# Column sums of a linear-attention kernel: one burst after each job, or one pair of matmuls after every second tile of the next job

## What is computed

```python
xn = layernorm(x)
q, k, v = split(xn @ W_qkv.T)            # 16 heads of 128
q = elu(q) + 1; k = elu(k) + 1
out = q * cumsum(k * v) / (q * cumsum(k) + 1e-9)     # over the 16,384 tokens
x = x + layernorm(out @ W_out.T * 128**-0.5)
# feed-forward, hidden 2048, inner 8192
f = silu((xn2 @ w_gate) * s_gate) * ((xn2 @ w_up) * s_up)    # xn2 = layernorm(x)
x = x + layernorm((f @ w_down) * s_down)
```

## Time and profile before

| | us |
|---|---|
| median of 2 runs | 10222.65 (10217.5 to 10227.79) |
| the profiled execution | 10219.21 |
| its span, core 0 (slowest) | 10217.6 |
| its span, core 4 (fastest) | 10086.5 |

### The profile page before, as it was taken

The page is one execution under the profiler, slowest core; times in us unless marked ns, Lnnn a source line. Parts: engine busy times, 40 slices in busy tenths (PEclk is TensorE's granted clock), DMA queues, the critical chain, the costliest instruction groups (busy, mean ns, idle before and its releaser), DMA issues.

```text
span 10217.6 us, 92396 instructions; the slowest of 8 cores (10086.5 to 10217.6 us)
## 1 busy us (share of the span) xinstructions
PE 7937.6 (78%) x33524; PEld 3392.3 (33%) x34200; DVE 2220.8 (22%) x3267; ACT 2050.9 (20%) x2825; POOL 492.5 (5%) x497
## 2 busy tenths in 40 slices
PE   0898687886868868688686885555599899899897
PEld 0343233332323323233232331111244344344343
DVE  3331231222313223132231111333210110210101
ACT  1222222222322323233231221121100000100100
POOL 0000000000000000000000000000011111111110
PEclk9999888888888888888887986666799999999998
DMA  4653433324333243332433113222697896995994
GB/s 114 147 115 59 111 82 72 83 53 100 81 75 85 59 97 82 70 87 63 97 82 62 26 26 78 87 87 80 107 153 148 165 152 150 162 157 155 157 145 140
DMA packets 1214500, 1034.29 MB, mean 101 GB/s; under 512 B 385330, under 2 KB 1089843, under 8 KB 1187123
## 3 DMA queue, kind: packets, MB, share of 16 engines
q0 software_dynamic: 759504, 587.23, 35.1%
q1 hardware_dynamic: 85412, 348.80, 9.8%
q10 hardware_dynamic: 369152, 92.31, 5.1%
HBM read 749.06 MB, written 153.35 MB: 88 GB/s over the span
## 4 chain that ended last, share of the span: by engine, by line
PE 73%; DMA 10%; ACTq 6%; ACT 4%; issue 3%; DVE 3%; another core or an unknown queue 1%; SPq 0%; DVEq 0%; POOLq 0%
PE psq L54 41%; PE ps_z L54 9%; PE ps_g L54 8%; PE ps_u L54 8%; DMA ts_st<-tsrow 6%; ACTq L54 6%; PE ps_at L54 2%; ACT tsrow L54 2%; PE ps_kvc L54 1%; PE ps_kc L54 1%; PE psts L54 1%; DVE ln_s L54 1%; DMA xb<-x_sh 1%; DMA q_st<-qbuf 1%
## 5 line engine op out<-in xcount | busy, mean ns | idle before, releaser
L54 PE MATMUL psq<-wqb,xnT 128*128 128x512 bf16 x19054 | 4274.1, 384 | 437.0 <-DMA xnT<-xn_st 372.6
L54 PEld LDWEIGHTS psq<-wqb,xnT 128*128 128x128 bf16 x19456 | 1921.1, 99 | 2808.2 <-issue 582.7
L54 PE MATMUL ps_g<-ynT,wgb 128*128 128x512 bf16 x4014 | 935.0, 383 | 154.7 <-DVE fuse L54 104.4
L54 PE MATMUL ps_u<-ynT,wub 128*128 128x512 bf16 x4014 | 919.9, 379 | 4.3
L54 PE MATMUL ps_z<-wdb,fuse 128*128 128x512 bf16 x4015 | 891.8, 382 | 33.9 <-DVE zf L54 19.7
L54 DVE SCALAR_TENSOR_TENSOR kbuf<-psq,r2b 128x512 bf16<-128x512 f32 x576 | 398.0, 691 | 2385.9 <-ACT r2b L54 2385.9
L54 ACT COPY tsrow<-psts 1x1024 f32<-1x1024 f32 x512 | 491.5, 998 | 1623.6 <-issue 776.9
L54 DVE SCALAR_TENSOR_TENSOR kvbuf<-psq,kbuf 128x512 bf16<-128x512 f32 x576 | 397.9, 691 | 1841.9 <-PE psq L54 1828.2
L54 PE MATMUL psts<-kvbuf,u_sb 128*1 128x512 bf16 x512 | 206.1, 520 | 696.2 <-ACT tsrow L54 695.5
L54 ACT ACTIVATE r2b<-psq 128x512 f32<-128x512 f32 x640 | 380.9, 595 | 1350.9 <-PE psq L54 1338.6
L54 PEld LDWEIGHTS ps_g<-ynT,wgb 128*128 128x128 bf16 x4096 | 403.9, 99 | 647.8 <-issue 175.1
(11 more groups left out here) (58 smaller groups left out, 2007.8 us busy)
## 6 DMA issues: line engine op xcount, KB each, us to landing
wqb<-wqkvT POOLq DMA_DIRECT2D x76, 2048.0 KB, 17.2
xb<-x_full SPq DMA_DIRECT2D x128, 1024.0 KB, 4.9
wgb<-wg POOLq DMA_DIRECT2D x128, 1024.0 KB, 6.9
wub<-wu POOLq DMA_DIRECT2D x128, 1024.0 KB, 9.3
wdb<-wd POOLq DMA_DIRECT2D x128, 1024.0 KB, 5.1
xn_st<-xnb SPq DMA_DIRECT2D x144, 512.0 KB, 2.8
xb<-x_sh SPq DMA_DIRECT2D x16, 1024.0 KB, 6.1
xrb<-x_sh SPq DMA_DIRECT2D x16, 1024.0 KB, 5.9
```

Source lines behind the costliest of these rows:

```text
L54: ins = getattr(e, meth)(*args, **kw)
```

## The change

The sums of a job are no longer recorded behind its tiles. Each group of two (two `psts` matmuls, the copy, the DMA) becomes a function that remembers its buffer, column and the two eviction counts it waits for, and is put on a list, `st.pending_ts`. In the next job, one group is taken from the list behind each tile after which `st.gidx` is odd, that is behind its tiles 0, 2, ..., 14; background steps stay behind the odd tiles. At the last job of a pass the whole list, which then holds that job's eight groups, is emptied after `tail_hook`. The waits of a group are the same, with the parity of the buffers taken when it is emitted. `P1State` gets a constructor.

```diff
--- before.py
+++ after.py
@@ -247,8 +247,10 @@
                 p0_tile(x_src, row0, tt, dst_st, xbuf, xnb, ln_done, dxp2, dxnp2)
 
         class P1State:
-            gidx = 0
-            ts_group = 0
+            def __init__(self):
+                self.gidx = 0
+                self.ts_group = 0
+                self.pending_ts = []
 
         mev_hist = {}
 
@@ -318,6 +320,8 @@
 
                     mev_hist[st.gidx] = mev_now
                     st.gidx += 1
+                    if st.pending_ts and st.gidx % 2 == 1:
+                        st.pending_ts.pop(0)()
                     if bg and st.gidx % 2 == 0:
                         bg.pop(0)()
 
@@ -326,17 +330,21 @@
                     tail_hook = None
                 if ts_base is not None and kind in ("k", "v"):
                     tbuf = kbuf if kind == "k" else kvbuf
-                    for tt in range(NTT):
-                        gpar = st.ts_group % 2
-                        TE.wait(C["mev"], mev_hist[st.gidx - NTT + tt])
-                        if tt % 2 == 0 and st.ts_group >= 2:
-                            TE.wait(C["mtse"], st.ts_group - 1)
-                        TE.op("matmul",
-                              ps_ts[gpar][0:1, (tt % 2) * 512:(tt % 2) * 512 + 512],
-                              u_sb[:, 127:128],
-                              tbuf[:, tt * 512:(tt + 1) * 512],
-                              start=True, stop=True, inc=(C["mts"], 1))
-                        if tt % 2 == 1:
+                    for t0 in range(0, NTT, 2):
+                        def ts_group_emit(t0=t0, tbuf=tbuf, kind=kind, col=col,
+                                          base=ts_base,
+                                          mevs=(mev_hist[st.gidx - NTT + t0],
+                                                mev_hist[st.gidx - NTT + t0 + 1])):
+                            gpar = st.ts_group % 2
+                            for j, tt in enumerate((t0, t0 + 1)):
+                                TE.wait(C["mev"], mevs[j])
+                                if j == 0 and st.ts_group >= 2:
+                                    TE.wait(C["mtse"], st.ts_group - 1)
+                                TE.op("matmul",
+                                      ps_ts[gpar][0:1, j * 512:j * 512 + 512],
+                                      u_sb[:, 127:128],
+                                      tbuf[:, tt * 512:(tt + 1) * 512],
+                                      start=True, stop=True, inc=(C["mts"], 1))
                             dtsp = C["dts0"] if gpar == 0 else C["dts1"]
                             SC.wait(C["mts"], C["mts"].n)
                             SC.wait(dtsp, dtsp.n)
@@ -345,14 +353,17 @@
                             st.ts_group += 1
                             SY.wait(C["mtse"], ev)
                             idx = 0 if kind == "k" else 1
-                            g0 = ts_base + tt - 1
                             SY.op("dma_start",
-                                  out=ts_st[idx:idx + 1, g0:g0 + 2,
+                                  out=ts_st[idx:idx + 1, base + t0:base + t0 + 2,
                                             col:col + 512],
                                   in_=tsrow[gpar][0:1, :].rearrange(
                                       "p (g j) -> p g j", j=512),
                                   inc=(dtsp, 16))
-
+                        st.pending_ts.append(ts_group_emit)
+
+                if ji0 == len(jt_list) - 1:
+                    while st.pending_ts:
+                        st.pending_ts.pop(0)()
                 if do_stash:
                     buf = {"k": kbuf, "v": kvbuf, "q": qbuf}[kind]
                     stg = {"k": k_st, "v": kv_st, "q": q_st}[kind]
```

## The result

| us | before | after |
|---|---|---|
| profiled execution | 10219.21 | 9410.47 |
| its span, slowest core | 10217.6 (core 0) | 9408.9 (core 2) |
| spans of the eight cores | 10086.5 to 10217.6 | 9383.0 to 9408.9 |
| lowest of all runs | 10204.51 (10 runs) | 9405.67 (11 runs) |
| median of all runs | 10516.53 | 9842.65 |

The ratio of after to before is 0.9206, 95% interval 0.9182 to 0.9231: 7.9% less time. Both medians hold executions in which the four cores of one die, or all eight, were granted a lower TensorE clock on average; the ratio and the times of the experiments leave these cores out.

A forecast was written before the change was run, and what follows sets the result against it. TensorE bound the kernel, idling before `psts` for copies `tsrow` and their DMAs. 10,219 − 1,023 (56 bursts) − 68 (cold restarts) + 278 (448 pairs) = 9,406 us; range 9,310 to 9,590.

The forecast's parts named there:

- a pair: Two `psts` matmuls after every second tile of the next job: 0.62 us each, 448 of them adding 278 us.
- switching: TensorE going from full matmuls to `psts` and back: 0.10 and 0.09 us per pair.
- a pass's end: Last job of a pass, sums still emptied behind the transposes: 66 us, unchanged; 465 us over eight stay.
- rival B: Inside passes, all cores dense: clock lowered; at 0.81 the whole gain of 813 us goes, near 10,220; chance 0.04.
- Rivals A and C: A: pairs dearer, 9,769 at 1.43 us each, chance 0.12. C: copy and DMA set the pace, 10,430 or more, 0.03.
- the ring: Copy into `tsrow`, then DMA out, two buffers: 14.1 us between uses against some 8.2 at worst, so nothing waits.
- Rival D: At a pass's end: transposes late for want of `xn_st`, at most some 57 us a pass, some 9,810; chance 0.03.
- The cover: Copies on ScalarE and DMAs on SP, moved into the next job, fit in slack: cost nothing, ScalarE about 41% busy.
- The sum: Profiled execution: 10,219 − 1,023 (56 bursts) − 68 (their cold restarts) + 278 (448 pairs) = 9,406 us.
- The spread: Across cores: core 0 stays slowest, core 4 gains some 80 us less, ending near 9,355; 131 narrows to about 50 us.
- cold restart: TensorE resuming at a lower clock after a burst inside a pass: 1.2 us each, 56 removed, 68 us.

## Why the prediction came out as it did

The mechanism and its size were right: at full clock the changed kernel takes 9,406 to 9,421 us, where 9,406 was forecast. The median of all runs, 9,843, is 253 us above the range.

| step | predicted | measured |
|---|---|---|
| a pair | 0.62 us | 0.627 |
| of it, switching | 0.19 | 0.20 (one matmul behind every tile) |
| a job with its pairs | 60.2 | 60.28 |
| a pass | 544 | 544.7 (1080.99 to 1625.65) |
| idle before `psts` | 420 | 411 |
| clock inside a pass | 0.98 or more | 1.00 |
| a pass's end | 66, unchanged | 65.0; across seven ends 121.7 against 121.8 |
| waits of copies for DMAs between tiles | none | none (24 waits, three at each flush) |
| slowest core, spread | core 0, 50 us | core 2, 26 us |

*The step that failed* is the one that made the sum into a forecast of the median: "the median of the runs shown is 10,223, 4 us above that execution, so I leave it at 9,406". It let three executions that agreed stand for all. The range was then built from the kernel's own mechanisms only. The clock entered as an outcome of the change (rival B, 0.04), not as something that befalls either kernel from one execution to the next, though it moves the changed kernel's time by up to 1,057 us (9,405.67 to 10,462.75). The runs show it in both kernels. Of the changed kernel 8 of 11 executions took 9,534 us or more, each with one die or both at a lower clock. Of before 5 of 10 took 10,780 or more; their clocks weren't kept, but executions of before beside the experiments show the same (11,574 us with all cores at 0.76 to 0.77). The median execution of the changed kernel shows both clocks side by side: cores 0 to 3 ran at a granted clock of 0.914 on average and ended at 9,391 to 9,403, cores 4 to 7 at 0.87 and ended at 9,814 to 9,841. The two medians, 10,517 and 9,843, stand at 0.936, where the ratio at full clock is 0.921.

*Rival B* as written, that density brings the lower clock and eats the gain, isn't borne out: in four executions of the changed kernel the average is 0.91, up from 0.875 to 0.88, and the own pass stays at 1.00. Whether density makes the lower clock more frequent, 8 of 11 and 5 of 10 can't tell. But the sentence that the trace of the own pass disagrees with the page was too strong. In another execution, of the kernel with one row buffer, the own pass of core 4 ran at 0.82, beside 0.99 at the same place before:

```profile
302.00:816.00 514.00, 507.20 (x1938) 210.44 (x1939) 160.19 (x248) 117.70 (x176) 7.99 (x7) 0.82 0.48 109
```

1,938 matmuls stand where before has 2,339. The Trainium skill, "TensorE: Matmul & The Clock Gate", Part 1, "Seeing it yourself", gives 13/16 (0.81) for dense matmuls on three or more cores of a die. This row agrees with the level. That it holds whenever three cores are dense doesn't agree: in the profiled execution of the changed kernel the same stretch is at 1.00 on each of the eight cores, all dense. What sets it off wasn't found.

*Rivals A and C* are closed: the switch was measured in two ways (one matmul behind every tile, four behind every fourth), and the ring has room even with half its buffers. *Rival D* didn't come: the passes' ends are as long as before.

*The cover* on which the moved copies were costed at nothing held. ScalarE is busy 147 us in 450, a third rather than the 41% worked out; the stretch holds four v jobs, which need it little, and three k jobs.

*The sum, and the luck in it.* The sum was made on core 0. There the eight passes, up to the first matmul of the prefix sums, took 5,120.1 us before (from 1079.81) and 4,308.0 after (from 1064.75): 812 less, where 813 was forecast. The first row is of before, the second of the changed kernel:

```profile
6199.86 8.35 PE L54 MATMUL ps_pre<-tssb,ps_sb 128*16 128x512 f32 x16 [11.78 <-DMA tssb<-ts_st]
...
5372.79 9.54 PE L54 MATMUL ps_pre<-tssb,ps_sb 128*16 128x512 f32 x16 [11.51 <-DMA tssb<-ts_st]
```

But core 0 ended at 9,384.2, some 20 us below the forecast, since its passes also began 15 us earlier and what follows them took 6 us less, neither of which the change touches; and the slowest was core 2, at 9,408.9. That the profiled time is only 4 us from the forecast is luck to that extent.

*The spread* was half seen. Core 4 had 80 us less of waits, but I had it keep its lead at the passes' ends. Before, these measure 119.3 us on it against 121.8 on core 0, its transposes taking 53.7 us on average; in the changed kernel they measure 122.2 and 56.3. That is 20 us over seven ends; another 10 came behind the passes. It gained 703 us, not 732.

## What to carry to other kernels

When a tiny result leaves by a chain of copy and DMA, the size of the result says nothing; count the round trips, and first see whether more buffers break them (two thirds of the gain here), and then hand the work to a place where the bound engine is busy anyway (the rest). The price of such a move is what the engine pays for switching, 0.2 us here, and can be read beforehand at the edges of the burst. A forecast of a median needs more than a few executions that agree: the three of before lay within 0.1%, and of ten, five were over 5% longer. A range built from one trace holds only for runs whose clock is like it.

## What the runs showed of the hardware

- A pause need not cost a cold restart, and the length of the burst alone doesn't decide it. In the run with eight row buffers the next job took 55.4 us (from 1150.94) after a burst of 10.6 us whose longest idle time was 3.5 us, and 56.8 us (from 1214.51) after one of 8.2 us whose longest was 0.9. The granted clock (third from the right) was 1.00 in the first of these jobs and 0.78 over the second burst and its edges. The bursts of the kernel before gave 56.6 us on average.

```profile
1151.00:1206.00 55.00, 54.74 (x251) 24.91 (x256) 20.08 (x32) 8.39 (x9) 0.00 (x0) 1.00 0.27 83
...
1204.00:1216.00 12.00, 9.46 (x30) 2.67 (x30) 5.09 (x4) 8.00 (x8) 1.15 (x1) 0.78 0.82 183
```

- A DMA transpose can hold the queue that issues it: 14.3 us for one of 1,024 tokens while a 2 MB `wqb` load was under way, about 1.4 us each in the half before it. Whatever stands behind it on that engine is held too.
- The same 16 transposes took between 48.9 us (core 4 of before) and 63.0 (two groups behind every fourth tile), and from 53.7 to 60.0 on average over the seven ends of a pass, without a change to them that would say why.
